# A recommendation tower on one core: id spreads ahead of the fetches, one wide pause write, layer 2 of the last round moved

## What is computed

```python
e = jnp.stack([tbl_0[ids[:, 0]], ..., tbl_25[ids[:, 25]]], axis=1)      # 2048 x 26 x 128
combined = jnp.concatenate([dense_features[:, None, :], e], axis=1)
interactions = jnp.einsum('bnd,bmd->bnm', combined, combined)
z = jnp.concatenate([dense_features, interactions[:, TRIU_I, TRIU_J]], axis=1)
h = jnp.concatenate([z, dense_features], axis=1)                        # 2048 x 607
h = jnp.maximum(h @ W_top1 + b_top1, 0.0)                               # 512
h = jnp.maximum(h @ W_top2 + b_top2, 0.0)                               # 256
y = h @ W_top3
```

## Time and profile before

| | us |
|---|---|
| median of 3 runs | 560.08 |
| lowest and highest | 558.93 to 563.88 |
| the profiled execution | 561.57 |
| its span | 560.0 |
| mean granted TensorE clock | 0.923 |

### The profile page before, as it was taken

The page is one execution under the profiler, slowest core; times in us unless marked ns, Lnnn a source line. Parts: engine busy times, 40 slices in busy tenths (PEclk is TensorE's granted clock), DMA queues, the critical chain, the costliest instruction groups (busy, mean ns, idle before and its releaser), DMA issues.

```text
span 560.0 us, 13448 instructions
## 1 busy us (share of the span) xinstructions
PE 482.8 (86%) x4385; PEld 433.1 (77%) x4385; DVE 364.0 (65%) x760; ACT 249.8 (45%) x750; POOL 419.9 (75%) x1291
## 2 busy tenths in 40 slices
PE   0667779789899989998999989998999899969866
PEld 0556678678797879887988889888988798859765
DVE  6656558877577747767676847776776677762630
ACT  2112244435544364536453644447443635374631
POOL 8999649796599979995999979996999799970000
PEclk9865578788999989999999989999999999988979
DMA  8941102111111111111111111111111111110000
GB/s 210 258 138 34 29 20 80 38 33 34 31 40 41 39 40 40 43 37 36 42 42 37 39 40 38 43 39 38 39 44 39 35 40 44 39 34 2 2 1 2
DMA packets 16650, 26.59 MB, mean 47 GB/s; under 512 B 8126, under 2 KB 10694, under 8 KB 16572
## 3 DMA queue, kind: packets, MB, share of 16 engines
q0 software_dynamic: 8192, 16.79, 11.4%
q1 hardware_dynamic: 8380, 8.83, 6.2%
HBM read 25.60 MB, written 0.01 MB: 46 GB/s over the span
## 4 chain that ended last, share of the span: by engine, by line
PE 62%; DVE 14%; issue 11%; ACT 11%; POOL 0%; ACTq 0%; DVEq 0%; POOLq 0%
PE fetch_ps L379 24%; PE dots_ps L356 17%; PE mlp_ps L413 11%; DVE onehot L686 7%; ACT vecs L545 4%; ACT inter L570 4%; DVE inter L744 4%; PE mlp_ps L422 3%; PE vec_ps L333 3%; PE ids_ps L364 3%; DVE t_lo L709 2%; ACT vecs L511 2%; PE mlp_ps L429 1%; ACT found L530 1%; DVE mask_f L718 0%
## 5 line engine op out<-in xcount | busy, mean ns | idle before, releaser
L295 POOL DMA_INDIRECT rows<-in_tbl,idx x256 | 251.1, 981 | 81.0 <-POOL unread L284 41.2
L686 DVE TENSOR_TENSOR onehot<-ids_ps,row_of 125x1024 fp32r<-125x1024 f32 (+1 forms) x162 | 200.1, 1276 | 96.3 <-PE ids_ps L364 76.3
L379 PE MATMUL fetch_ps<-onehot,t_hi 125*128 125x256 f32 x672 | 190.5, 312 | 31.0 <-DVE t_lo L709 24.7
L379 PE MATMUL fetch_ps<-onehot,t_lo 125*128 125x256 f32 x672 | 189.0, 310 | 0.0
L379 PEld LDWEIGHTS fetch_ps<-onehot,t_hi 125*128 125x128 f32 x672 | 138.3, 206 | 40.6 <-DVE t_lo L709 27.8
L284 POOL MEMSET unread<- 128x126 f32 x1024 | 165.6, 220 | 0.1
L744 DVE COPY_PREDICATED inter<-mask,dots_ps 27x64 f32<-27x64 int32 (+2 forms) x512 | 106.3, 208 | 70.6 <-ACT inter L570 55.6
L379 PEld LDWEIGHTS fetch_ps<-onehot,t_lo 125*128 125x128 f32 x672 | 138.2, 206 | 10.2 <-issue 2.5
L570 ACT COPY inter<-dots_ps 27x64 f32<-27x64 f32 (+1 forms) x512 | 102.5, 200 | 70.0 <-PE dots_ps L356 51.4
L356 PE MATMUL dots_ps<-vecs 128*64 128x54 f32 x2048 | 127.4, 228 | 2.3 <-ACT vecs L511 2.3
L356 PEld LDWEIGHTS dots_ps<-vecs 128*64 128x64 f32 x2048 | 122.3, 143 | 8.5 <-ACT vecs L511 2.5
(11 more groups left out here) (45 smaller groups left out, 222.1 us busy)
## 6 DMA issues: line engine op xcount, KB each, us to landing
rows<-in_tbl,idx POOLq DMA_INDIRECT x256
vecs<-in_tbl SPq DMA_DIRECT2D x8, 448.0 KB
rows<-in_r_dense_features SPq DMA_DIRECT2D x16, 64.0 KB
h_sb<-in_W_top_laid SPq DMA_DIRECT2D x2, 512.0 KB
found<-in_tbl SPq DMA_DIRECT2D x1, 560.0 KB
h_sb<-in_tbl SPq DMA_DIRECT2D x1, 560.0 KB
w_sb<-in_W_top SPq DMA_DIRECT2D x1, 512.0 KB
vecs<-in_tbl SPq DMA_DIRECT2D x8, 52.0 KB
```

The source lines that it names most:

```text
L295: nc.gpsimd.indirect_dma_start(out=rows[v % 2][:, s, :], out_offset=None, in_=tables[f - 1][:, :], in_offset=bass.IndirectOffsetOnAxis(ap= ...
L379: last = pe.matmul(fetch_ps, part[0:KP, T0[k] + h * KH[k] + t, :], onehot[buf][h][0:KP, t, :], start=(h == 0 and t == 0 and part is t_hi), ...
L686: dve.tensor_tensor(onehot[buf][h][0:KP, 0:kh], ids_ps[0:KP].rearrange("p (o r) -> p o r", o=1).to_broadcast([KP, kh, R]), rows_at[0:KP, h ...
```

## The change

In PE's first round the spread of item k+1 moves out of the fetch of item k to a place before it, behind a wait for both compares of item k. The pause of POOL becomes one memset of 512 numbers on 64 partitions, into partitions 64 to 127 of `ids_i`, which is made 128 partitions tall (its ids and results lie on partitions 0 to 41); `unread` and `ones` go, and `ident` is set to one and masked in place. In `layer1` the wait for `x_lo` stands before the eleventh matmul of the first output instead of before the first. In `last_step` both outputs of layer 2 come behind the transposes of group 2, and groups 3 and 4 behind them; ScalarE's order follows.

```diff
-        unread = sb("unread", [P, 4, 126])
-        ones = unread[:].rearrange("p a b -> p (a b)")[:, :P]
...
-        ids_i = sb("ids_i", [32 + X, B // 2], I32)
+        ids_i = sb("ids_i", [P, B // 2], I32)
+        unread = ids_i[64:P, 0:4 * P].bitcast(F32)
...
-            PARTS = 4
-            PAUSES = PARTS * (NR - 1)
+            PAUSES = NR - 1
...
-                    pool.wait_ge(pauses_made, i * (4 * PAUSES) + v * PAUSES + n * PARTS)
+                    pool.wait_ge(pauses_made, i * (4 * PAUSES) + v * PAUSES + n)
                 pool.sem_inc(pauses_begun, 1)
-                for part in range(PARTS):
-                    pool.memset(unread[:, part, :], 0.0).then_inc(pauses_made, 1)
+                pool.memset(unread, 0.0).then_inc(pauses_made, 1)
...
-            pool.memset(ones, 1.0).then_inc(ones_set, 1)
-            pool.wait_ge(ones_set, 1)
-            pool.affine_select(out=ident[:], in_=ones, compare_op=ALU.is_equal, fill=0.0, base=0,
+            pool.memset(ident[:], 1.0).then_inc(ident_set, 1)
+            pool.wait_ge(ident_set, 1)
+            pool.affine_select(out=ident[:], in_=ident[:], compare_op=ALU.is_equal, fill=0.0, base=0,
...
                         pe.wait_ge(x_hi_made, tiles)
-                        pe.wait_ge(x_lo_made, tiles)
...
                             jj, w, x = at - 2 * (JG + 1), w_hi, x_lo
+                            if m == 0 and jj == 0:
+                                pe.wait_ge(x_lo_made, tiles)
...
                     for k in range(X):
-                        pe.wait_ge(lo_made, k + 1)
+
+                        pe.wait_ge(compared, k * 2 + 2)
                         if k == X - 1:
                             pe.wait_ge(ids_cast, 2)
-                        fetch(k, k, k % 2, ((k + 1) // X, (k + 1) % X, k + 1))
+                        spread_ids((k + 1) // X, (k + 1) % X)
+                        pe.wait_ge(lo_made, k + 1)
+                        fetch(k, k, k % 2)
...
                 layer1(i, 0, 3)
-                transpose_rows(i, 3, (2, 3, 4))
+                transpose_rows(i, 3, (2,))
                 layer2(i, 0, 0)
+                layer2(i, 0, 1)
+                transpose_rows(i, 3, (3, 4))
                 dots(i, 3, 0)
-                layer2(i, 0, 1)
                 layer3(i, 0)
...
-                take_vectors(i, 3, 2, 4)
-                rectify2(i, 0, 0)
+                take_vectors(i, 3, 2)
+                rectify2(i, 0, 0, 1)
+                take_vectors(i, 3, 4)
                 take_products(i, 3, 0)
-                rectify2(i, 0, 1)
                 take_products(i, 3, 1)
```

More of the change, by code:

```diff
@@ L145, in dlrm_tower @@
         mlp_ps = [ps(f"mlp_ps{m}", [P, 512])[:, 0:R] for m in range(2)]
-        ones_set = sem("ones_set")
+        ident_set = sem("ident_set")
         ident_made = sem("ident_made")
```

## The result

The changed kernel takes 539.19 us (median of 4 runs, 538.78 to 540.92) against 559.56 for the kernel before: ratio 0.9626, 95% interval 0.9573 to 0.9680. The forecast was 543.7 with a range of 537.5 to 551.

What follows compares the result with a forecast made beforehand. PE bounds the loop, and a ring of waits through PE and VectorE the opening, with POOL not bounding. Terms of -17, -0.9 and +1.5 sum to -16.4 us, taking 560.08 to 543.7 us, range 537.5 to 551.

Steps and rivals of the forecast that it cites:

- Part 1: Opening: spread ahead of the fetch lets it run while VectorE splits, ending the ring of PE and VectorE; gain 17 us.
- POOL's stand: POOL's waits for PE's transposes, 10.53 us before the third tile and 8.35 before the fifth, would supply the 17 us.
- Which level?: PE's clock in the opening: expected to swing between 1.2 GHz (gain 12.7 us) and 2.4 GHz (23.2), so 17.
- rival B: PE's clock stays at 2.4 GHz in the opening: gain 23.2 us, total 537.5; chance 0.17.
- comparison of two loads: Opening: at 2.4 GHz PE has 2.5 us of work in 3.5, again 71%, a share that had not held the clock.
- Part 2: POOL's pause as one memset of 512 on 64 partitions: 535 ns, 0.11 us gained per gather, worth nothing in total.
- the slower rival: POOL becomes the bound: with the wide memset from 0.84 us the kernel is over 1% slower; chance 0.02.
- Part 3: Last round's layer 1: PE starts behind x_hi, waiting for x_lo only after ten matmuls; gain 0.9 us.
- Part 4: Last round: both layer 2 halves before two transpose groups; PE then stands some 2 us for VectorE's merges; loss 1.5 us.
- The sum: Whole kernel: -17 -0.9 +1.5 = -16.4 us, taking the median from 560.08 to 543.7.

Runs made afterwards that it cites:

- the repeat: The changed kernel run unchanged once more, on one chip beside the kernel with layer 2 put back: 540.39 us (8 runs).
- part 1 alone: The kernel before with only the first round's spreads moved ahead of the fetches, the four memsets kept as pause: 536.82 us, ratio 0.9552.
- VectorE held up: The changed kernel with two memsets of 512 numbers added on VectorE behind the splits of items 2 to 6 of the first round: 544.89 us, one execution.
- layer 2 put back: The changed kernel with the last round's layer 2, and ScalarE's order, back where they were: 535.19 us, ratio 0.9529; run once more, 536.99 us.
- the other order of the end: The changed kernel with the last round's dots(3,0) first, then both layer 2 halves, dots(3,1), layer 3; ScalarE keeps y: 535.6 us, ratio 0.9533.

## Why the prediction was right, and where it was off

**Part 1** was right in mechanism: VectorE's wait of 2.70 us is gone, its own chain of compares and split became the bound at 3.40 us per item (3.5 forecast), nothing in the loop gave any of it back (417.2 to 423.8 us between the marks in three profiles with the old opening, 418.3 to 423.8 in ten with the new one), and POOL's stand covered the shift. The term that was mis-sized is the gain, 17 forecast and 23.04 measured, and within it the step "Which level?". The forecast lay between a gain of 12.7 at the one level and 23.2 at the other; it chose 17, and the total fell into the range only because the low end of the range was this second case. The tenth fetch ended at 51.8 (its copy starts at 51.83), where I had 51.6 for 2.4 GHz from the second fetch on and 62.1 for 1.2 GHz: rival B, to which I gave 0.17, is what happened. That the two times agree within 0.2 us is partly luck: in this profile the second fetch still ran at the low level (starts 0.21 us apart until 24 us), so the third began at 24.80 and not at 23.4, and items of 3.40 us instead of 3.5 made up for it. In the repeat the level rose within the first fetch, the third began at 22.38, and the first mark is 1.4 us earlier.

The step that was off is the comparison of two loads. I set PE's 71% at the new pace and 2.4 GHz beside the 71% of the old pace at 1.2 GHz and called them the same load. They are not: the busy time of one item is 4.4 us at the one level and 2.5 at the other for the same 17 matmuls. Sorted by how far the items are apart, the runs are in order: 3.4 us apart the clock stayed at 1.00 (changed kernel, part 1 alone), 4.8 apart it was 0.50 (VectorE held up), 6.2 apart 0.50 in 42 to 56 us (before). By busy share they are not in order: 75%, 81%, 74%. The one item of the new opening that comes 4.6 us behind the one before, the ninth, lies between: behind it the level fell in the profile of layer 2 put back (0.87 in 42 to 56 us) and in five others, and stayed in those of the changed kernel and of part 1 alone. Whether the pace or the length of the stands decides is not shown, since each of these runs changes both.

**Part 2**: 546 ns for 535, and worth nothing that the times show, as forecast; the slower rival lies where it was put.

**Part 3** was forecast at 0.9 us and measured 0.6 to 0.7 in the ends. I had put layer 1's first ten matmuls at 0.12 us each; they run at 1.2 GHz (starts 0.21 us apart), with either place of the wait, and starting them earlier only lets more of them run there. The 1.0 us won at the start becomes 0.6 at the end.

**Part 4** was forecast as a loss of 1.5 us from the wait for VectorE's merges, and that step stands: counted from the last transposes of group 2, dots(3,1) start 12.2 us later in the changed kernel (498.57 to 510.80) and 10.8 with layer 2 back (496.17 to 506.99), 1.4 us. But the whole loss is 3.04, because I left out the clock: the dots behind the stand of 2.33 us take 5.25 us instead of 3.75, which is the other 1.5. This is no chance of one execution: all seven profiles with the new order that have this stand (2.15 to 2.34 us) have 5.20 to 5.25 us for these dots, and all six with the old order, without the stand, have 3.75. I had only added durations from before, where PE did not stand there.

**The sum**: -17-0.9+1.5 = -16.4 was forecast, -23.0-0.6+3.0 = -20.6 measured. Both errors, 6.0 and 1.5 us, are about the clock and of opposite sign, so the total is nearer to the forecast than the first of them. Even so 539.19 lies under the 540.5 to 547 to which I gave 0.52, nearest to rival B's 537.5. The four per cent from part 1 hide a loss of half a per cent, which only a kernel without part 4 brings out.

## What to carry to other kernels

A small producer step for the next item, standing inside a long step that itself waits for the previous item, ties two engines into one ring; moved ahead of that wait, it lets each run at its own pace. Here the pace was then that of the slower engine, VectorE, with TensorE's clock at the full level from the second or third fetch on, but for a few microseconds behind the ninth in some profiles. Busy shares of TensorE taken at different clock levels are not the same measure, since the same 17 matmuls were busy for 4.4 us at the low one and for 2.5 at the full one: before setting two of them side by side, look at the granted clock of each, and count the matmuls too. When filler work is moved on TensorE, look for the wait that it had been filling: a stand of 2.3 us there was followed by dots that took 1.5 us longer, as much again as the 1.4 us that the wait itself had cost. And read a local change in its own stretch of the profile: the stretch between the marks alone varies by up to 6.6 us from one profile to the next.

## What was unexpected

- The clock fell behind short stands: 2.33 us before dots(3,1), and in the other order of the end two stands of 0.86 and 0.68 us around a few transposes were followed by dots of 5.28 us, though the same 0.86 us with layer 2 behind the transposes (old order) left the dots at 3.75. What decides between these two stays open.
- A pause write reduced to one number left gathers and total unchanged. Whatever reason the pauses have, it is not time in this kernel.
- The kernel before varies more from run to run (554.12 to 565.89 us in one series of 17) than the one with layer 2 back (534.88 to 535.6 and 535.48 to 538.5 in two series of 6), though another kernel with the new opening also spreads by 5.8 us in a series of 6 (531.71 to 537.55, the other order at the end). In three profiles with the old opening the granted clock of its 14 us windows between 28 and 70 us lay between 0.50 and 0.74 and not in the same places, which may be one reason; no run was made to test that.
